# One transposing DMA per token tile, row scales from magnitude sums, and new orders for all engines in a sandwich layer

## The reference, cut to what matters

```python
def phi(x): return elu(x) + 1.0
def attn(x, W_qkv, W_out):                  # x (4, 1024, 512), 16 heads of 32
    q, k, v = split(x @ W_qkv.T, 3)
    q, k = phi(q), phi(k)
    kv_cumsum = cumsum(k * v, axis=tokens)  # in each channel by itself
    k_cumsum  = cumsum(k, axis=tokens)
    return (q * kv_cumsum / (q * k_cumsum + 1e-9)) @ W_out.T * 32 ** -0.5
def ffn(x, w_gate_up, w_proj):              # (4096, 512) and (512, 2048)
    gate, up = split(x @ ternary(w_gate_up).T)
    return rms_norm(silu(gate) * up) @ ternary(w_proj).T
# ternary(w): bf16; in groups of 64 elements w / mean|w| is rounded, clipped to -1, 0, 1, scaled back
x = x + layernorm(attn(layernorm(x)))
x = x + layernorm(ffn(layernorm(x)))
```

## Time and profile before

| | before |
|---|---|
| median of 3 runs | 1176.94 us (1176.35 to 1178.77) |
| the profiled execution | 1178.05 us |
| its span, first to last instruction | 1176.3 us |
| mean granted TensorE clock | 0.966 |
| PE busy | 1069.3 us, 91% |
| DVE busy | 793.6 us, 67% |
| POOL busy | 522.0 us, 44% |
| ACT busy | 477.1 us, 41% |

### The profile page before, as it was taken

One profiled execution on the slowest core, in us unless ns is written; L12 is line 12 of the kernel. 1 busy time (PEld: TensorE's weight loads), 2 busy tenths in 40 slices (PEclk: granted clock), 3 DMA queues, 4 the chain that ended last, 5 costly groups with the idle time before them and its releaser, 6 DMA issues. The chain is left out here.

```text
span 1176.3 us, 14162 instructions
## 1 busy us (share of the span) xinstructions
PE 1069.3 (91%) x5088; PEld 522.7 (44%) x5088; DVE 793.6 (67%) x1236; ACT 477.1 (41%) x788; POOL 522.0 (44%) x474
## 2 busy tenths in 40 slices
PE   1859677999999898999999998999999998999997
PEld 1325344455444353446444453446444453454443
DVE  5878989987567759653885379743985379626424
ACT  2543657565442114441344324441344324433433
POOL 1235658887735333442544243442544243415322
PEclk9879889999999998999999999999989998999999
DMA  7541143520031223020220123011210221101000
GB/s 213 130 104 45 46 135 99 153 64 19 1 78 66 40 68 72 1 37 20 73 52 1 36 72 72 1 37 32 72 40 1 37 72 36 36 1 37 36 1 36
DMA packets 104197, 63.82 MB, mean 54 GB/s; under 512 B 76480, under 2 KB 84672, under 8 KB 104128
## 3 DMA queue, kind: packets, MB, share of 16 engines
q1 hardware_dynamic: 102256, 59.52, 20.0%
q10 hardware_dynamic: 1872, 3.41, 0.8%
HBM read 34.60 MB, written 9.44 MB: 37 GB/s over the span
## 5 line engine op out<-in xcount | busy, mean ns | idle before, releaser
L599 PE MATMUL bank<-x3t,wgu_t 128*128 128x512 f16 x1536 | 361.2, 390 | 30.7 <-DMA x3t<-x3s 28.6
L599 PEld LDWEIGHTS bank<-x3t,wgu_t 128*128 128x128 bf16 x1536 | 151.2, 100 | 221.5 <-issue 29.0
L1267 POOL TENSOR_TENSOR acc<-acc,ht 128x512 f32<-128x512 f32 x90 | 115.0, 1278 | 260.2 <-ACT ht L995 259.3
L632 PE MATMUL bank<-wproj_t,hid 128*128 128x512 bf16 x872 | 202.6, 379 | 1.7 <-ACT wproj_t L867 1.7
L588 PE MATMUL bank<-xnt,wqkv_hi 128*128 128x512 f16 x672 | 165.0, 390 | 21.0 <-issue 13.4
L1628 DVE TENSOR_TENSOR ht<-ht,bank 128x512 f32<-128x512 f32 x112 | 75.8, 677 | 130.6 <-PE bank L599 110.6
L983 ACT ACTIVATE hid<-ht 128x512 f16<-128x512 f32 x109 | 68.5, 629 | 167.1 <-DVE ht L1628 167.0
L632 PEld LDWEIGHTS bank<-wproj_t,hid 128*128 128x128 f16 x872 | 85.0, 98 | 103.6 <-issue 2.6
L1634 DVE TENSOR_TENSOR hid<-ht,hid 128x512 f16<-128x512 f32 x109 | 84.1, 771 | 65.2 <-ACT hid L983 65.1
L1219 POOL TENSOR_TENSOR tk<-tq,ts 128x512 f32<-128x512 f32 x28 | 52.1, 1862 | 160.4 <-DVE ts L1554 107.7
L588 PEld LDWEIGHTS bank<-xnt,wqkv_hi 128*128 128x128 f16 x672 | 66.4, 100 | 105.1 <-issue 31.5
(11 more groups left out here) (180 smaller groups left out, 1522.6 us busy)
## 6 DMA issues: line engine op xcount, KB each, us to landing
raw_q<-in_L_ffn_w_gate_up_dram SPq DMA_DIRECT2D x32, 256.0 KB, 2.9
...
```

The source lines that it names most:

```text
L599: last = pe.matmul(bank[:], wgu_t[:, k, first_row:first_row + P], x3t_of(f)[:, part, k], start=(n == 0), stop=(n == 2 * KD - 1))
L632: last = pe.matmul(bank[:], hid_of(f, part, k)[:, t * P:(t + 1) * P], wproj_t[:, k], start=(k == 0 and part == 0), stop=(k == MT - 1 and p ...
L1267: pool.tensor_tensor(acc[:], acc[:], ht_of(f)[:, m % 2], ALU.add).then_inc(q["acc_done"], 1)
```

## The change

- `xs` and `x3s` lie token tile by token tile (`[P, NT, 2, KD, P]`), and each token tile, both halves together, is transposed by one DMA of 8 blocks: four DMAs per chunk instead of two, the same number of blocks. PE still waits for the whole chunk.
- Chunk 1's x gets buffers of its own (`xn_b`, `xs_b`) and is loaded right behind the first loads; before, it was loaded into `xn` once chunk 0 had left it.
- The power of two for a row of `W_qkv` comes from the sum of its magnitudes instead of the largest one. The sum of channel tile 0 is a `tensor_reduce` on DVE as before; those of tiles 1 to 3 are nine `activation`s on ACT with `accum_out`. The powers are made in three steps (tile 0, 1, 2 and 3) instead of two.
- The first channel tile is transposed by six DMAs of 4 blocks (q, k, v, high and low), and `group(0, g)` waits only for its part.
- All weights are loaded from SP, before mostly from ACT. The layer norm of chunks 0 and 1 (`norm_tile`) runs on POOL, before on ACT. `weight_lo` of tiles 2 and 3 runs on POOL, as two instructions each, before as one on DVE.
- The orders of all engines, in `start()`, `step()` and `last_steps()`, are new.

```diff
-        xs = sb("xs", [P, 2, KD, NT, P], FP16)
+        xs = sb("xs", [P, NT, 2, KD, P], FP16)
-        x3s = sb("x3s", [P, 2, KD, NT, P], FP16)
+        x3s = sb("x3s", [P, NT, 2, KD, P], FP16)
+        xn_b = sb("xn_b", [P, NT, D], F32, at_x3t)
+        xs_b = sb("xs_b", [P, NT, 2, KD, P], FP16, at_ring)
...
-            def turn(x, split, part, ready, count, done):
-
-                sp.wait_ge(ready, count)
-                sp.dma_start_transpose(x[:, part].rearrange("p k (t n) -> p (k t) n", n=P),
-                                       split[:, part].rearrange("p k t n -> p (k t n)")).then_inc(done, 16)
...
+            def turned_tile(x, t):
+
+                return x[:].rearrange("p a k n -> p (a k) n")[:, :, t * P:(t + 1) * P]
...
+            def turn_x3(f, *tiles):
+
+                for t in tiles:
+                    if t == 0 and f > 1 and f < NC - 1:
+                        sp.wait_ge(FF_MAIN["gate_done"], MT * ffn(f)[1])
+                        sp.wait_ge(FF_MAIN["up_done"], MT * ffn(f)[1])
+                    sp.wait_ge(x3s_hi, at(NT, f, t))
+                    sp.wait_ge(x3s_lo, at(NT, f, t))
+                    sp.dma_start_transpose(turned_tile(x3t_of(f), t), x3s[:, t].rearrange("p a k n -> p (a k n)")).then_inc(x3t_done, 16)
...
+            def turn_first_weights(*parts):
+
+                for part in parts:
+                    sp.wait_ge(w_hi, part + 1)
+                    sp.dma_start_transpose(wqkv_hi[:, 0, part], wsplit[0][:, 0, part]).then_inc(wt_first[part], 16)
+                    wait_low_weights(sp, 0, part)
+                    sp.dma_start_transpose(wqkv_lo[:, 0, part], wsplit[0][:, 1, part]).then_inc(wt_first[part], 16)
...
+                load_first_x(2), load_first_raw(2, 1, 0), load_first_x(0, 1, 3), load_x(1), load_raw(1, 2, 3)
...
-                    if m == 0 and k == 0:
-                        pe.wait_ge(x3t_lo if part else x3t_hi, 16 * (f + 1))
+                    if m == 0 and n == 0:
+                        pe.wait_ge(x3t_done, 16 * NT * (f + 1))
...
+            def weight_sum(j, *parts):
+
+                for part in parts:
+                    wait_weights_in(act, j, part)
+                    act.activation(magnitudes[3 * (j - 1) + part][:], raw_a[j][:, part], ACT.Abs,
+                                   accum_out=peak[:, j, part:part + 1]).then_inc(w_peak_b, 1)
...
+            def weight_lo(j, *parts):
...
+                    pool.tensor_scalar(raw_a[j][:, part], raw_a[j][:, part], enlarge[:, j, part:part + 1], None, ALU.mult).then_inc(w_scaled, 1)
+                    pool.wait_ge(w_scaled, 3 * (j - 2) + part + 1)
+                    pool.tensor_tensor(wsplit[j % 2][:, 1, part], raw_a[j][:, part], wsplit[j % 2][:, 0, part], ALU.subtract).then_inc(w_lo_b, 1)
```

More of the change, by code:

```diff
@@ L374, in own_instruction, with powers_for, wait_low_weights, wait_weights_in @@
             eng.sem_inc(passed_pool if eng is nc.gpsimd else passed_dve, 1)
+        def powers_for(j):
+            return min(j, 2) + 1
+        def wait_low_weights(eng, j, part):
+            if j < 2:
+                eng.wait_ge(w_lo, 3 * j + part + 1)
+            else:
+                eng.wait_ge(w_lo_b, 3 * (j - 2) + part + 1)
+        def wait_weights_in(eng, j, part):
+            eng.wait_ge(raw_first_in[part] if j == 0 else raw_a_in[j - 1], 16)
+        def wait_turned_weights(eng, j):
+            if j == 0:
+                for part in range(3):
+                    eng.wait_ge(wt_first[part], 32)
+            else:
+                eng.wait_ge(wt_hi[j - 1], 16)
+                eng.wait_ge(wt_lo[j - 1], 16)
         def single_of(f):
@@ L775, in start @@
-                gate_unit(1, 14), up_unit(1, 14), gate_unit(1, 15), up_unit(1, 15), group(2, 0, 1, 2), square_sums(1)
-                group(2, 3, 4, 5), project(1, 0, 1, 2, 3, 4, 5), group(2, 6, 7, 8), project(1, 6, 7), group(2, 9, 10, 11)
-                project(1, 8, 9, 10, 11, 12, 13), project(1, 14)
-                project(1, 15), group(3, 0, 1), project_att(2, 0, 1, 2, 3), group(3, 2)
-            def step(s, first):
-                group(s, *range(first, 12))
-                f = s - 1
-                for m in range(MT):
-                    gate_unit(f, m), up_unit(f, m)
-                    if m >= 3:
-                        project(f, m - 3)
-                project(f, 13, 14, 15), project_att(s, 0), square_sums(f), project_att(s, 1, 2, 3)
@@ L1190, in rstd_power @@
                 pool.wait_ge(q["var_s"], 2 * (c + 1))
+                if which == "1" and c > 0:
+                    pool.wait_ge(xn1_ready, NT * c)
                 pool.tensor_tensor(q["rstd"][:], q["var"][:], mhalf[:].to_broadcast([P, NT]), ALU.pow).then_inc(q["rstd_s"], 1)
@@ new lines, in start @@
+                back_output(0, 0), weight_lo(3, 1), back_lo(0, 0), weight_lo(3, 2), den_product(0, 1), num_product(0, 1)
+                den_product(0, 2), back_output(0, 1), back_lo(0, 1), num_product(0, 2), back_output(0, 2), back_lo(0, 2)
+                den_product(0, 3), num_product(0, 3), divide(0, 1), back_output(0, 3), den_product(1, 0), back_lo(0, 3)
+                divide(2), num_product(1, 0), power_lead(0), power_rest(0), back_output(1, 0), back_lo(1, 0)
+                scale_back(0), power_take(0), den_product(1, 1), rstd_power("2", 0), num_product(1, 1)
@@ L1507, in stats_mean @@
                 dve.wait_ge(q["stats_s"], 2 * NT * (c + 1))
+                if which == "1" and c == 1:
+                    dve.wait_ge(q["nb_s"], 1)
                 dve.tensor_scalar(q["nm"][:], q["mv"][:, :, 0], -1.0, None, ALU.mult).then_inc(q["var_s"], 1)
@@ new lines, in start @@
+                sum_values(1, 2), back_reciprocal(1, 2), feature_k(1, 3), scale_row(4), scale_rec(5)
+                front_products(1, 3), scale_sums(6), diff(4), carry_value(1, 2), sum_keys(1, 3), hidden_value(0, 0)
+                scale_max(6), sum_values(1, 3), scale_row(5), carry_key(1, 3), back_output(1, 2), carry_value(1, 3)
+                back_reciprocal(1, 3), scale_bound(2), back_output(1, 3), back_lo(1, 2), scale_rec(6), back_lo(1, 3)
+                hidden_value(0, 1), clip(5), scale_sums(7, 8), scale_max(7), hidden_lo(0, 0), clip(6)
@@ new lines, in start @@
+                back_reciprocal(2, 2), feature_k(2, 3), feature_q(2, 3), front_products(2, 3), carry_key(2, 2)
+                sum_keys(2, 3), sum_values(2, 3), x_lo(3, 0, 1), carry_value(2, 2), x_lo(3, 2), back_output(2, 2)
+                carry_key(2, 3), x_lo(3, 3), back_reciprocal(2, 3), back_lo(2, 2), carry_value(2, 3), back_output(2, 3)
+                stats_tile("f", 1, 0, 1, 2, 3), stats_join("f", 1, 0, 1, 2, 3), stats_mean("f", 1), stats_var("f", 1)
+                back_lo(2, 3), add_final_tile(1, 0, 1, 2, 3), stats_tile("2", 2, 0, 1, 2, 3)
@@ new lines, in step @@
+                hidden_value(f, 11), hidden_lo(f, 10), carry_value(s, 3), back_reciprocal(s, 3), back_output(s, 3)
+                hidden_lo(f, 11), hidden_value(f, 12), x_lo(s + 1, 0), back_lo(s, 2), hidden_value(f, 13)
+                hidden_lo(f, 12), hidden_lo(f, 13), hidden_value(f, 14), x_lo(s + 1, 1), back_lo(s, 3), x_lo(s + 1, 2)
+                hidden_lo(f, 14), hidden_value(f, 15), hidden_lo(f, 15), stats_tile("f", f, 0, 1, 2, 3)
+                stats_join("f", f, 0, 1, 2), stats_tile("2", s, 0), read_square_sums(f), x_lo(s + 1, 3)
```

762 lines of the change are left out of this document (417 added, 345 removed).

## The result

The changed kernel takes 1150.7 us (median of 4 runs, 1149.28 to 1151.67) against 1176.99: a ratio of 0.9773, 95% interval 0.9756 to 0.979. It is 26 us faster where 58 were forecast, and lies above the range.

The account below looks back on a forecast made before the run. PE, busy 91% of the span, was taken to bound the kernel, its 107 us of standing still being the prize, with the start DVE's. Savings of 20 + 2 + 10 + 26 = 58 off 1178.05 gave 1120 us, range 1100 to 1146.

Parts of the forecast that it names:

- Part A: Start, up to chunk 0's x3: less DVE work and less idle time save 20 us, bounds 14 to 26.
- scaled to busy time, 107.0: Start: DVE's new list at the old trace's means, 115.3 us instead of 121.4, scaled to 107.0 busy, 5.7 less.
- Part B: Weight stretch, 152 to 330 us: PE waits for single weight tiles; saves 2 us, between -5 and +9.
- four batches are finished instead of two, so the transposes find their tiles ready: Weight stretch: more batches done at chunk 0's x3, so PE's transposes wait less often; behind the +2 us.
- The rival that named the start's loss: Start's gain lost at POOL through late `weight_lo`, holding up DVE's chunk 0: 39 us off, 1139 us, chance 0.17.
- Part C: Chunks 2 and 3: earlier x split removes stalls of 2.7 and 5.7 us and slow matmuls; saves 10, between 6 and 11.
- Part D: Five x3 waits of chunks 2 to 6, 32 us with slow matmuls: earlier split saves 26, between 16 and 31.
- T: In each step, the end of `project_att(f, 3)`, from which the race between PE's request and x3's landing is timed.
- The take-back of 1.2 us a step: Steps: allowance for PSUM and `hidden_value` coming due while DVE is behind, 6 us in all.
- The second price of a stall: Matmuls behind a PE wait run slower: 8 take 3.57 us, where 8 behind no wait take 1.90.
- rival (5): Change is slower: a chunk's four DMAs don't overlap, each with its own 4.2 us landing; 1203 us, chance 0.05.
- rivals (3) and (4): (3): start's gain lost at POOL, 1139 us, chance 0.17; (4): steps' units run into DVE, 1136 us, chance 0.06.

Follow-up runs that it names:

- pool_small: Changed kernel with POOL's two products per weight batch cut to 64 of 1024 columns and DVE's clip reading the weights, for measuring only: 1118.06 us.
- port_probe: Separate kernel, computing nothing of the reference: eight kinds of DVE instruction alone and beside POOL products; four DVE products take 2.87 us alone, 5.70 beside POOL.
- pool_small_before: Kernel before with POOL's two products per weight batch cut to 64 columns and DVE's clip reading the weights: 1178.09 us against 1179.77.
- lo_on_dve_b: Changed kernel with the low halves of weight channel tiles 2 and 3 made on DVE instead of POOL: 1147.31 us against 1148.66 for the changed kernel.
- new_steps: Kernel before with one transposing DMA per token tile and the changed orders of steps 3 to 6 and last steps, old start: 1153.99 us, ratio 0.9782.
- tiles_only: Kernel before with one transposing DMA per token tile instead of one per half, all orders as they were: 1179.05 us, ratio 0.9999.

## Why the prediction was wrong

**Bound and mechanism.** That PE's stalls are the prize, that the start is DVE's and that an earlier x3 split pays in each step held. The total failed, 29 us short by the spans, and 21 of these lie in A and B, where the prediction priced DVE's new list at the means of the old trace.

**Part A, 20 forecast, 11.2 measured: the step "scaled to busy time, 107.0".** The pieces around it were near. The first group started at 23.66 (22.7 forecast), `group(1, 0)` at 69.5 without a stall of its own (61 forecast), and DVE's idle time up to the last `x3_lo` was 135.9 - 121.2 = 14.7 us, less than the 20 assumed. But DVE was busy 121.2 us, not 107.0. The excess in this stretch is 15.4 us larger than before (24.4 against 9.0), enough to cover the 14.2 us between 107.0 and 121.2; pool_small, with an unaltered list on DVE, gives 10.9 of it back and ends this part 8.4 us earlier. POOL was busy 94.3 us up to there instead of 57.0. The prediction added up POOL's 14.8 us for the low halves and asked only who waits for POOL; it did not ask whom POOL's reading stops. Those twelve instructions took 21.1 us:

```profile
L1304 POOL TENSOR_SCALAR raw_a<-raw_a,enlarge 128x512 f32<-128x512 f32 x6 | 13.1, 2184 | 0.6 <-ACT wsplit L893 0.6
L1306 POOL TENSOR_TENSOR wsplit<-raw_a,wsplit 128x512 f16<-128x512 f32 x6 | 8.0, 1330 | 0.5
```

That is 3.5 us a pair, above the 2.5 that the prediction had named as a sign of being wrong. The `tensor_scalar` had been priced at 0.925 by `norm_tile`, another form; port_probe has 1.56 for this one. For the fourth channel tile, forecast on time, PE waited 3.69 us: its last low half ended on POOL at 56.69, the transpose was issued at 56.72, and PE went on at 60.45. For the third it waited 3.59 us, not 2.

**Part B, +2 forecast (-5 to +9), -10.4 measured.** The step "four batches are finished instead of two, so the transposes find their tiles ready" failed: DVE, at 80% busy taken for free, went to 87%: the excess is 20.0 us larger (44.8 against 24.8) at like count, and PE waited 14.6 us for `diff` in this stretch. pool_small shows the price: with POOL's reading for the weight batches almost gone this stretch is 25 us shorter and PE is 98% busy. In the kernel before, the same cut gained nothing (pool_small_before): the price belongs to the new order, in which PE waits for a DVE that POOL holds up. The rival that named the start's loss, 1139 us, put it down to `weight_lo` alone; with that gone the time hardly moves (lo_on_dve_b), so of the single rivals its figure came nearest to 1150.7, but by the wrong cause.

The rule was in the Trainium skill, page "SBUF — State Buffer", section "Who interferes with whom": DVE and GpSimd share one pair of ports as an exclusive lock, taken by a DVE instruction in a two-port mode, or by one with two SBUF inputs against a GpSimd instruction that reads. The rows above agree: the product with a PSUM operand, statistics and sums are untouched (2.85, 2.88 and 2.85 us for four), products, scans and bf16 clips are held up (5.70, 7.63 and 5.74 against 2.87, 5.00 and 1.81), and fills nearly spare `diff` (0.80 us) but not the clip (0.90). The prediction looked for rules on DMAs and on POOL's speed, and not for one on the pair of engines that the change loads most.

**Part C, 10 forecast, 8.1 measured.** The stalls of 2.7 and 5.7 us went; in their place came one of 2.75 for `xnt` and one of 1.56 at `project_att(2)`, more than the 0.5 allowed. It stayed within its bounds.

**Part D, 26 forecast, 20.1 measured**, in its range, and shown to stand by itself (new_steps). PE asked at T + 28.7 (28.5 forecast), the last split ended at T + 25.5 (25.1). It landed at T + 30.0 instead of 28.2: the sum gave a tile 3.1 us to land, which is right (3.2 measured from its issue), but not SP's four issues of 1.3 us in a row, so that the last one left 1.1 us after its split. That is 4.5 us behind the split, past the 4 that the prediction had named as its sign. The take-back of 1.2 us a step was a wait for a bank, of 1.17 and 1.12 us in two steps and 0.48 in a third; together with waits of 1.3 to 2.5 for x3 and some small ones the steps kept 12 us of stalls, not 6. Of the 32 us at stake 12 stayed, which leaves about the 20.1 measured. The second price of a stall did go: behind a wait of 1.2 us, 64 matmuls take 13.99 us, 0.219 each, where 60 took 14.44 to 16.07. The rival (5), DMAs one behind the other, was wrong; that the four DMAs do nothing by themselves, as tiles_only shows, was not among the rivals.

**What the chances missed.** All four estimates came out too high. A and B lean on one price list, that of the old trace, so they failed together, and D fell short of its figure for reasons of its own. The prediction had worked out 1155 for rivals (3) and (4) together, near to what was measured, but left it out of its range.
